# Fused cross-attention and top-2 mixture of experts: hC cleared on GpSimd, VectorE's and ScalarE's last attention slot put behind the first expert group, scatters that wait for one landing, the last chunk routed in two slots

## The reference, cut to what matters

```python
x = x + cross_attention(layernorm(x), ctx_768)     # 64 batches of 128 rows x 128; 16 heads of 64; 77 keys of 96
n = layernorm(x).reshape(-1, 128)                  # 8192 rows
logits = n @ router_w.T                            # 8 experts
_, idx = top_k(softmax(logits), 2)
gate = zeros(T, 8).at[rows, idx].add(take_along_axis(logits, idx))
for e in range(8):
    moe += gate[:, e:e+1] * ((silu(n @ w1[e].T) * (n @ w3[e].T)) @ w2[e].T)
moe += (silu(n @ sw1.T) * (n @ sw3.T)) @ sw2.T     # the shared expert
x = x + moe
```

## Time and profile before

| | us |
|---|---|
| median of 3 runs | 1050.55 |
| lowest, highest | 1046.46, 1054.25 |
| the profiled execution | 1049.61 |
| its span in the profile | 1047.7 |
| PE busy | 948.9 (91%) |
| DVE busy | 837.6 (80%) |
| POOL busy | 748.1 (71%) |
| ACT busy | 647.4 (62%) |

### The profile page before, as it was taken

One profiled execution on the slowest core, in us unless ns is written; L12 is line 12 of the kernel. 1 busy time (PEld: TensorE's weight loads), 2 busy tenths in 40 slices (PEclk: granted clock), 3 DMA queues, 4 the chain that ended last, 5 costly groups with the idle time before them and its releaser, 6 DMA issues.

```text
span 1047.7 us, 28760 instructions
## 1 busy us (share of the span) xinstructions
PE 948.9 (91%) x9838; PEld 799.4 (76%) x9838; DVE 837.6 (80%) x1904; ACT 647.4 (62%) x1354; POOL 748.1 (71%) x1121
## 2 busy tenths in 40 slices
PE   7899999999999999999999999988699999999910
PEld 6677778788878788778778787866499999987710
DVE  5898989989999998999899999899455556656721
ACT  4676779877777777767777777766234444453300
POOL 5345546767778778767877877887644588888887
PEclk9999999999999999999999999998799999999965
DMA  9154223253342323322434434254346576677421
GB/s 269 47 167 105 51 47 70 46 145 70 62 80 57 82 60 71 70 57 58 82 78 83 79 59 81 60 138 88 75 136 184 156 194 183 169 169 151 141 89 60
DMA packets 222733, 106.55 MB, mean 102 GB/s; under 512 B 160464, under 2 KB 214384, under 8 KB 221456
## 3 DMA queue, kind: packets, MB, share of 16 engines
q1 hardware_dynamic: 214400, 87.91, 35.9%
q0 software_dynamic: 8192, 16.79, 5.9%
HBM read 38.59 MB, written 34.60 MB: 70 GB/s over the span
## 4 chain that ended last, share of the span: by engine, by line
PE 38%; DVE 33%; POOL 13%; issue 9%; ACT 4%; DMA 3%; SPq 0%; DVEq 0%; POOLq 0%; ACTq 0%
POOL ctx_raw L582 9%; DVE top L983 7%; DVE pt_lo L1024 6%; DVE P L993 6%; PE Q L1273 5%; PE W L1137 3%; PE W L1138 3%; POOL ctx_raw L592 3%; PE W L1139 3%; PE S L1205 3%; DVE v_lo L1000 3%; PE W L1381 2%; PE S L1260 2%; PE W L1382 2%; DMA OT_lo<-O_lo 2%
## 5 line engine op out<-in xcount | busy, mean ns | idle before, releaser
L529 POOL TENSOR_TENSOR O_lo<-O,O_hi 128x512 f16<-128x512 f32 x128 | 145.6, 1157 | 162.8 <-ACT O_hi L696 162.8
L1024 DVE TENSOR_TENSOR pt_lo<-Q,pt_hi 77x512 f16<-77x512 f32 x256 | 164.0, 679 | 38.3 <-ACT pt_hi L688 37.5
L478 POOL DMA_INDIRECT xs<-x2cat,pos x128 | 133.0, 1039 | 61.7 <-DMA xs<-x2cat,pos 30.9
L688 ACT ACTIVATE pt_hi<-Q 77x512 f16<-77x512 f32 x256 | 144.4, 589 | 28.0 <-PE Q L1273 27.5
L664 ACT ACTIVATE v_hi<-W,sc 77x512 f16<-77x512 f32 x128 | 87.7, 686 | 117.2 <-PE W L1139 116.4
L1273 PE MATMUL Q<-ident,P 128*77 128x128 f32 x1024 | 148.3, 278 | 2.2 <-ACT P L671 0.8
L582 POOL DMA_INDIRECT ctx_raw<-ys,pos_y x128 | 132.1, 1032 | 23.3 <-issue 21.2
L1205 PE MATMUL S<-G,xTm 128*128 128x462 f32 (+1 forms) x384 | 143.2, 508 | 0.0
L1260 PE MATMUL S<-v_hi,pt_hi 96*128 96x65 f16 x1024 | 109.8, 197 | 28.9 <-DVE P L993 25.9
L1260 PEld LDWEIGHTS S<-v_hi,pt_hi 96*128 96x128 f16 x1024 | 93.9, 97 | 49.5 <-DVE P L993 44.5
L1273 PEld LDWEIGHTS Q<-ident,P 128*77 128x77 f32 x1024 | 122.1, 149 | 3.5 <-issue 2.4
(11 more groups left out here) (256 smaller groups left out, 2902.8 us busy)
## 6 DMA issues: line engine op xcount, KB each, us to landing
ys<-ysb SPq DMA_DIRECT2D x44, 256.0 KB
xg_early<-xs SPq DMA_DIRECT2D x60, 128.0 KB
xp<-x2cat SPq DMA_DIRECT2D x64, 64.0 KB, 1.9
y_out<-X SPq DMA_DIRECT2D x16, 256.0 KB
xg_late<-xs SPq DMA_DIRECT2D x28, 128.0 KB
xs<-zero_in SPq DMA_DIRECT2D x24, 128.0 KB, 2.5
X<-x_in SPq DMA_DIRECT2D x1, 2240.0 KB, 8.2
xs<-x2cat,pos POOLq DMA_INDIRECT x128, 3.0
```

The source lines that it names most:

```text
L478: pool.indirect_dma_start(out=xs_d[batch_part(b)][:, :], out_offset=index(pos, b, k), in_=x2cat[:, b % RING, :], in_offset=None).then_inc( ...
L529: pool.tensor_tensor(O_lo[:, half_], O[:, (t + 1) % 2, half_], O_hi[:, half_], ALU.subtract).then_inc(s["p_Olo"], 1)
L688: act.activation(pt_hi[0:NK, j % 2, c * 512:(c + 1) * 512], QB[q_bank(j, c)][0:NK, :], ACT.Copy).then_inc(s["a_PThi"], 1)
L1024: dve.tensor_tensor(pt_lo[0:NK, j % 2, c * 512:(c + 1) * 512], QB[q_bank(j, c)][0:NK, :], pt_hi[0:NK, j % 2, c * 512:(c + 1) * 512], ALU.s ...
```

## The change

Six edits:

- hC is cleared by POOL after its slot 64, where it waits for the last scores (`s_S`), and no longer by DVE. hC and hA change places in memory.
- DVE and ACT run slot 65 behind group 0's work instead of before it (`range(FIRST, LAST)` and no `n > 0`).
- PE's last projection moves from group 1 to group 0.
- Scatters have a semaphore for each of the two DMAs, in rings of 8. Above slot 65 a batch waits only for the first DMA of the batch before; in all slots from the ninth batch on it waits for both of eight batches ago.
- The last chunk (7) is chosen in slots 69 and 70, two pieces each, instead of 69 to 72, and is placed in slot 71 instead of 73.
- The tables of part 2 begin two slots earlier (73 instead of 75).

```diff
         HR = 3
+        hC = sb("hC", [128, HR, NT])
         hA = sb("hA", [128, HR, NT])
-        hC = sb("hC", [128, HR, NT])
...
-        TAB_SLOT = [CB * c + S_PLACE + 2 for c in P_END]
+        TAB_SLOT = [CB * c + S_PLACE + 2 - (2 if c == NCH - 1 else 0) for c in P_END]
...
+        SOONER = 2
+        PLACE_AT = {CB * c + S_PLACE - (SOONER if c == NCH - 1 else 0): c for c in range(NCH)}
+        CHOOSE_AT = {}
+        for c in range(NCH):
+            for k in range(4):
+                CHOOSE_AT.setdefault(CB * c + S_CHOOSE + (k // 2 if c == NCH - 1 else k), []).append((c, k))
...
         def scattered(eng, b):
-            wait(eng, f"sc{b % RING}", 32 * (b // RING + 1))
+            for k in range(2):
+                wait(eng, f"sc{k}_{b % SCR}", 16 * (b // SCR + 1))
...
                     if t > LAST:
-                        scattered(pool, b - 1)
+                        wait(pool, f"sc0_{(b - 1) % SCR}", 16 * ((b - 1) // SCR + 1))
+                    if b >= SCR:
+                        scattered(pool, b - SCR)
                     scatter(b, 0); scatter(b, 1)
...
             for t in range(FIRST, LAST + 1):
                 slot(t)
+                if t == NB:
+                    pool.wait_ge(s["s_S"], 3 * NB)
+                    pool.memset(hC[:, :, :].rearrange("p r n -> p (r n)"), 0.0).then_inc(s["hC_zero"], 1)
...
-            for t in range(FIRST, LAST + 1):
+            for t in range(FIRST, LAST):
                 slot(t)
...
-                if n > 0 and LAST + n <= TAIL:
+                if LAST + n <= TAIL:
                     slot(LAST + n)
...
-            dve.memset(hC[:, :, :].rearrange("p r n -> p (r n)"), 0.0).then_inc(s["hC_zero"], 1)
...
-                if n == 1:
+                if n == 0:
                     project(LAST)
```

More of the change, by code:

```diff
@@ L36 @@
 RING = 16
+SCR = 8
 K_RANK = 0
@@ L205, in program @@
                  "xg0 xg1 xg2 xg3 xg4 xg5 st_y0 st_y1 st_y2").split()
-        names += [f"sc{r}" for r in range(RING)] + [f"xp{r}" for r in range(4)] + [f"ga{r}" for r in range(YR)]
+        names += [f"sc{k}_{r}" for k in range(2) for r in range(SCR)] + [f"xp{r}" for r in range(4)] + [f"ga{r}" for r in range(YR)]
         s = {n: sem(n) for n in names}
@@ L233, in x_bank @@
             return QB[(5 * t + 2) % 2] if t < NB else QB[1]
-        def chunk_of(t, first):
-            c = (t - first) // CB
-            return c if (t - first) % CB == 0 and 0 <= c < NCH else None
+        SOONER = 2
[4 more added lines that the diff above has]
+                CHOOSE_AT.setdefault(CB * c + S_CHOOSE + (k // 2 if c == NCH - 1 else k), []).append((c, k))
         def turns(t):
-            return on(t + 1, 0, NB), on(t - 4, 0, NB), on(t - 5, 0, NB), chunk_of(t, S_PLACE) is not None
+            return on(t + 1, 0, NB), on(t - 4, 0, NB), on(t - 5, 0, NB), t in PLACE_AT
         def turn_count(t):
@@ L478, in scatter @@
                 pool.indirect_dma_start(out=xs_d[batch_part(b)][:, :], out_offset=index(pos, b, k), in_=x2cat[:, b % RING, :],
-                                        in_offset=None).then_inc(s[f"sc{b % RING}"], 16)
+                                        in_offset=None).then_inc(s[f"sc{k}_{b % SCR}"], 16)
             def scatters(t):
@@ L531, in slot @@
             def slot(t):
-                if chunk_of(t, S_PLACE) is not None:
-                    members(chunk_of(t, S_PLACE))
+                if t in PLACE_AT:
+                    members(PLACE_AT[t])
                 if on(t, -1, NB - 1):
@@ L560, in slot @@
                     logits_out(t)
[L561 to L564, removed]
+                if t in PLACE_AT:
+                    place(PLACE_AT[t], t)
+                if t - 1 in PLACE_AT:
+                    place_picks(PLACE_AT[t - 1])
                 if on(t, S_W13 + 2, S_W13 + 6):
@@ L640, in turn_out @@
                 if hi == T_END:
-                    wait(act, "p_base", chunk_of(t, S_PLACE))
+                    wait(act, "p_base", PLACE_AT[t])
                 act.activation(xTm[:, (t + 1) % 2, lo:hi], x_bank(t)[:, lo:hi], ACT.Copy).then_inc(s["a_xT"], 1)
@@ L1040, in slot @@
                     moments(t)
-                for piece_ in range(4):
-                    if chunk_of(t, S_CHOOSE + piece_) is not None:
-                        choose(chunk_of(t, S_CHOOSE + piece_), piece_)
+                for c, k in CHOOSE_AT.get(t, []):
+                    choose(c, k)
                 if t == -1:
@@ L1173, in turn @@
                 if pre:
-                    c = chunk_of(t, S_PLACE)
+                    c = PLACE_AT[t]
                     if c == 0:
```

## The result

| | us |
|---|---|
| changed kernel, median of 18 runs | 1046.52 |
| lowest, highest | 1043.01, 1048.01 |
| the profiled execution, its span | 1047.98, 1046.1 |
| kernel before, median of 18 runs beside it | 1051.41 (1046.46 to 1056.56) |
| ratio, 95% interval | 0.9954 [0.9939, 0.997] |

What follows compares the result with a forecast made beforehand. The end was the first gather's start plus 214.6 us, gated by scatters or part 0's stores. First gather 833.1 to 830.9, 2.2 us off: 1047.4 from the profiled execution, 1048.3 from the median; said 1048.0, range 1044.5 to 1051.9 widened by 1 below, 0.6 above.

Steps and rivals of the forecast that it cites:

- The two gates: Before the first gather: scatters' end (833.1) and landing of part 0's last store (831.8), 1.3 us apart; gather moves to 830.9.
- The scatters: GpSimd's scatters wait for one landing, end at about 825, then hide behind part 0's stores; their gain stops at 1.3 us.
- the 13 waits: GpSimd's scatter waits for a landing; each shrinks by up to 1.3 us, 16.9 us in all.
- The hand-over: 733 to 757 us: PE starts 3.0 us sooner, its turn(LAST) ends 1.7 later, x2cat and part 0's stores come 1.3 sooner.
- turn 67: PE's turn with the last x2f, at 757.58 before; forecast 756.3, and after 758.9 the slower rival would decide.
- The clock: PE in the hand-over: projection and turn at 2.4 GHz save 1.8 us; low clock costs about 2 us per following group.
- Chunk 7: Last chunk's choice and placing two iterations sooner: put at nothing, upper bound 1.0 us if `p_M` comes late for PE.
- The train: GpSimd's unbroken run of gathers to the end: unchanged at 207 us, so the end follows the first gather's start.
- the slower one: Rival, chance 0.15: PE's projection in group 0 waits for the residual behind hA; first gather up to 835.4, end 1051.9.
- "No change": Rival, chance 0.12: first landing hardly sooner or scatters wait for `p_pos`; scatters end near 832.8, first gather 833.1, time 1049.6.

Runs made afterwards that it cites:

- e5: The kernel before, run again unedited for a second profile: 1052.69 us, ratio to itself 0.9989; the profiled execution took 1049.86 us.
- e4: Changed kernel with hC cleared one slot sooner on GpSimd, behind slot 63: 1045.47 us, ratio 0.9922 to the kernel before.
- e3: Kernel before with only the hand-over edits (hC cleared by GpSimd, slot 65 behind group 0, last projection in group 0): 1047.71 us, ratio 0.9968.
- e11: Changed kernel once more, unedited, on a fourth, slower chip: 1067.78 us, ratio 0.998 to the kernel before on that chip.
- e2: Changed kernel, but above slot 65 each scatter again waits for both landings of the batch before: 1054.31 us, ratio 1.001 to the kernel before.
- e6: Kernel before with only the chunk 7 edit (chosen in two slots, placed two slots sooner): 1054.53 us, ratio 1.0001.
- e8: Changed kernel with hC cleared one slot sooner and the 128 scalings moved from GpSimd to VectorE, its schedule retuned: 1004.49 us, ratio 0.9526 to before.
- e10: Changed kernel without the scatters' wait for the batch before, the wait for eight batches ago kept: 1089.92 us, ratio 1.0201 to the kernel before.

## Why the prediction was right, and where it was not

- **The two gates**: right. The last store, forecast for 827.8 (829.08 less 1.3), went out at 828.02. Landing and wake-up took 3.06 us, forecast 3.12, in each of the kernels whose first gather waited for this store. First gather 831.08, forecast 830.9; GpSimd's wait 9.92 us, forecast about 10.
- **The scatters**: the direction right, the price wrong. They ended at 821.2 instead of "about 825": their end came 11.6 us sooner, out of the 16.9 that the 13 waits could give. The step that failed is that their end was read from one execution and carried into the sum: "the two gates are only 1.3 us apart" held in that one and in e5's, both some 2 to 3 us below the median. The gain of this term was to be what the 1.3 us allow; the scatter edit alone measured 3.8 us in the medians (1.2 to 5.9 by its interval). But the hand-over, put at 1.3, alone measured as much (3.4, 0.8 to 6.0). The sum took 2.2 us off where 4.9 were to be had, and the runs don't say which of the two terms lacks the rest. That the forecast still came within 1.5 us is in part luck: it started from a profiled execution 1.8 us below the median of the kernel before.
- **The hand-over**: right nearly row for row. Forecast and found: second transposition 734.95, 735.30; clearing done 739.7, 739.8; residual L872 at 741.2, 741.40; projection 741.7, 741.80; x2cat 746.1, 746.13 and 751.6, 751.61; turn 67 at 756.3, 756.25. Put behind one another, the waits give 1.3 us; from the common start it is 1.46 at turn 67 and 1.19 at the last store. That x2cat and turn 67 agree within 0.1 us has luck in it, as the start of an execution moves by more than that. One term was off and hidden: the first `up` products ran at 2.4 GHz and were issued by 737.6, not 739.6, and PE only waited longer for the residual. In 742 to 746 us the granted clock was 0.50, which is 1.2 GHz, as assumed for the projection.
- **The clock**: before ran the first `up` at low clock; after ran `up` high and the projection low, e4 most of `up` low and the projection high. The prediction left this open between two bounds. The Trainium skill (TensorE: Matmul & The Clock Gate, "What's actually happening") says that the monitor isn't aligned to the kernel's start. The traces are divided on what the prediction drew from it, another clock from run to run: e3, with the changed kernel's instructions on PE in this stretch, ran most of `up` low and the first part of the projection high. But the kernel before had the same order in both its profiles (before, e5), and the changed kernel too (after, e11). No run here shows one program changing its clock at another point.
- **Chunk 7**: "nothing" was right for the time, and the reason was not. The edit was to be free because VectorE had room and `p_M` came early. In fact VectorE's choice comes late for GpSimd:

```profile
776.23 0.32 POOL L458 TENSOR_TENSOR mh<-pk 128x64 f16<-128x64 f32 x1 [4.33 <-DVE pk L911]
```

  PE's turn didn't wait for it, where the prediction had allowed up to 1.0 us. It costs nothing because the scatters end 9.9 us ahead of the first gather. Where they wait for both landings that cover is gone, and the executions profiled in e2 and e6 ended their scatters 5 us late. e2 against e3 makes a cost there likely; e6's own ratio, 1.0001, doesn't confirm it.
- **The train**: right, 206.2 against 205.8 us.
- **The rivals**: the slower one needed turn 67 after 758.9, and it came at 756.25. "No change" needed scatters near 832.8. The price of moving the residual behind hA, its mechanism, is real all the same: with the clearing out of hC's way (e4) turn 67 was 3.1 us sooner, 1.2 of them clock; with the projection back in group 1 1.5 to 1.9.

## What to carry to other kernels

Where two gates release the same instruction, their distance in one profile is one sample: if a gate ends a chain of many waits for DMA landings, ask for the spread of the times before taking the distance as the size of the gain. Follow an operation that is moved to another engine to whoever waits for it, since the clearing left VectorE's program and still held it for 3.3 us. Ask also what else hangs on what you move: the hand-over was meant for the stores and moved the scatters by 2 us as well. And when the end is a fixed train behind a start, a change at the start gives microseconds and one instruction less per step of the train gives the rest.

## What the runs showed of the hardware

- Indirect DMAs that GpSimd issues without a pause (0.96 us each and a gap of 0.30) can keep TensorE and SyncE from issuing: PE busy 4.97 of 20 us, a SyncE store 18.5 us behind the one before. With a wait for one landing per pair PE was busy 27.66 of 29 us on the same chip. One chip, one profile; what carries the effect is open.
- The same sign differs by chip. On two of four, PE idled beside gathers with scalings between them (24.89 of 36 us busy, 35.84 in the same kernel on another chip), and the kernel before took 17 to 20 us more there, the changed kernel 21. On a third chip e8's gathers, one every 1.25 us, left PE busy for 160 of 160 us. That it is one cause with the starving in e10 is not shown.
- Clearing 128 x 1536 f32 took 1.37 us on GpSimd and 1.34 on VectorE.
